# Adding scaled scan states with accumulating transfers instead of GpSimd additions, in a one-core two-layer block kernel

## The reference, cut to what matters

```
dA  = exp(delta[..., None] * A)            # 512 tokens x 512 channels x 16 states
dBu = (delta * u)[..., None] * B_ssm[:, :, None, :]
h   = dA_i * h + dBu_i                     # along the tokens
y   = einsum('bds,bs->bd', h, c_i)         # sum over the 16 states, each scaled by C
y   = y + u * D_param
```

## Time and profile before

| | |
|---|---|
| time, median of 3 runs | 3368.53 us (3368.17 to 3368.85) |
| profiled execution, its own time | 3364.8 us |
| its span, first to last instruction | 3362.8 us |
| granted TensorE clock, mean share of full speed | 0.928 |
| batches with the scan | from about 150 to 2700 us |
| expert part | from about 2785 us to the end |

### The profile page before, as it was taken

One profiled execution on the slowest core, in us unless ns is written; L12 is line 12 of the kernel. 1 busy time (PEld: TensorE's weight loads), 2 busy tenths in 40 slices (PEclk: granted clock), 3 DMA queues, 4 the chain that ended last, 5 costly groups with the idle time before them and its releaser, 6 DMA issues. The chain is left out here.

```text
span 3362.8 us, 46770 instructions
## 1 busy us (share of the span) xinstructions
PE 2834.9 (84%) x12696; PEld 1870.1 (56%) x12697; DVE 2546.5 (76%) x4108; ACT 2064.1 (61%) x3786; POOL 2592.0 (77%) x2474
## 2 busy tenths in 40 slices
PE   3686979797979797888888888888887779999998
PEld 2444555555555555555555555565545447777776
DVE  3498989899989989898999898989897842222222
ACT  3576677676767676766767676767665514444443
POOL 1399898989889898989898989898999913444444
PEclk7897989898989898989999999999998889999999
DMA  2001111111111111111110101010112313333333
GB/s 75 23 32 32 36 44 36 43 39 39 39 39 41 38 39 40 46 33 46 34 51 26 51 29 51 29 48 31 43 36 82 101 56 58 63 63 63 62 62 52
DMA packets 113898, 155.37 MB, mean 46 GB/s; under 512 B 15472, under 2 KB 73264, under 8 KB 113712
## 3 DMA queue, kind: packets, MB, share of 16 engines
q1 hardware_dynamic: 77344, 109.32, 10.4%
q0 software_dynamic: 25728, 34.75, 6.4%
q10 hardware_dynamic: 10640, 9.09, 0.8%
HBM read 107.36 MB, written 45.76 MB: 46 GB/s over the span
## 5 line engine op out<-in xcount | busy, mean ns | idle before, releaser
L872 POOL TENSOR_TENSOR dbu<-du,bbc 128x512 f32<-128x512 f32 x1024 | 1294.2, 1279 | 74.5 <-DVE h L1440 67.8
L1440 DVE TENSOR_TENSOR_SCAN h<-bank,dbu 128x512 f32<-128x512 f32 x1024 | 1227.3, 1212 | 158.7 <-ACT bank L1082 101.9
L1082 ACT ACTIVATE bank<-region,amat 128x512 f32<-128x512 f32 x1024 | 703.6, 691 | 313.3 <-DVE h L1440 299.0
L665 PE MATMUL bank<-ident,h 128*128 128x128 f32 x4096 | 624.9, 289 | 259.5 <-DVE acc L1430 231.4
L665 PEld LDWEIGHTS bank<-ident,h 128*128 128x128 f32 x4096 | 495.6, 148 | 544.3 <-DVE acc L1430 224.7
L858 POOL TENSOR_TENSOR acc<-acc,hTc 128x512 f32<-128x512 f32 x480 | 609.6, 1271 | 103.7 <-ACT hTc L1066 102.1
L1607 POOL DMA_INDIRECT out<-ye,ids x136 | 213.3, 1569 | 347.1 <-DMA out<-ye,ids 311.3
L1066 ACT ACTIVATE hTc<-bank,cT 128x512 f32<-128x512 f32 x480 | 327.3, 682 | 236.6 <-PE bank L665 236.5
L1430 DVE SCALAR_TENSOR_TENSOR acc<-bank,cT,acc 128x512 f32<-128x512 f32 x544 | 395.0, 730 | 38.9 <-PE bank L665 33.4
L619 PE MATMUL bank<-x4T,w_su 128*128 128x512 f32 (+1 forms) x768 | 389.2, 610 | 10.7 <-DVE score L1305 10.7
L1643 DVE SCALAR_TENSOR_TENSOR gg<-gt,bank 128x352 f32<-128x352 f32 x136 | 70.7, 520 | 382.2 <-ACT gt L1577 382.2
(11 more groups left out here) (204 smaller groups left out, 4361.1 us busy)
## 6 DMA issues: line engine op xcount, KB each, us to landing
bbc<-b_scratch SPq DMA_DIRECT2D x256, 256.0 KB, 3.1
xe<-slots_in SPq DMA_DIRECT2D x136, 129.0 KB
region<-in_x SPq DMA_DIRECT2D x16, 512.0 KB, 3.8
out<-x ACTq DMA_DIRECT2D x16, 512.0 KB, 3.1
region<-in_e_gu SPq DMA_DIRECT2D x8, 704.0 KB, 5.4
out<-ye,ids POOLq DMA_INDIRECT x136
slots_in<-dbu SPq DMA_DIRECT2D x16, 129.0 KB, 3.2
slots_in<-x,pos POOLq DMA_INDIRECT x128
```

Of the source, the lines that this page charges most:

```text
L665: last = tr(scan[f"hT{s}.{t}"][:, m * P:(m + 1) * P], h[:, s % 2, m, t * P:(t + 1) * P], ident[:, :])
L872: g.tensor_tensor(dbu[:, n % 4, :], du[:, m, :], bbc[:, (b * NS + s) % NROW, :], ALU.mult).then_inc(S("dbu_ready"), 1)
L1082: f(db(n)[:, :], delta[:, 1 - par, m, :], ACT.Exp, scale=amat[:, m, s:s + 1]).then_inc(S("da_ready"), 1)
L1440: v.tensor_tensor_scan(h[:, s % 2, m, :], db(n)[:, :], dbu[:, n % 4, :], 0.0, ALU.mult, ALU.add)\
```

## The change

Each of POOL's 30 additions per batch becomes a transfer from `hTc` to `acc` with `accum_op=ALU.add`. POOL issues it, the DMA engines read both and write the sum. Its completion adds 16 to one of two semaphores, one per `hTc` buffer, in place of the single counter `acc_added`. Every wait for an addition is turned into a wait for the landing of its transfer; the same engines wait at the same places.

```diff
+        acc_added = [sem(f"acc_added{k}") for k in range(2)]
+        PER_BUFFER = [(len(POOLED) + 1 - k) // 2 for k in range(2)]
+
+        def added(eng, b, k):
+            count = b * PER_BUFFER[k % 2] + k // 2 + 1
+            eng.wait_ge(acc_added[k % 2], 16 * count)
...
             elif (s - 1, t) in POOLED:
-                done(eng, "acc_added", b, POOLED.index((s - 1, t)))
+                added(eng, b, POOLED.index((s - 1, t)))
...
                     if m == 0:
                         done(pe, "acc_ready", b)
-                        done(pe, "acc_added", b)
+                        for k in range(2):
+                            pe.wait_ge(acc_added[k], 16 * (b + 1) * PER_BUFFER[k])
...
                     done(pool, "scaled", b, k)
                     acc_before(pool, b, s, t)
-                    g.tensor_tensor(acc[:, t, :], acc[:, t, :], hTc[:, k % 2, :], ALU.add).then_inc(S("acc_added"), 1)
+                    g.dma_start(acc[:, t, :], hTc[:, k % 2, :], accum_op=ALU.add).then_inc(acc_added[k % 2], 16)
...
                     scan.filled(act, f"hT{s}.{t}", b)
-                    before(act, "acc_added", b, k - 1)
+                    if b + k // 2:
+                        act.wait_ge(acc_added[k % 2], 16 * (b * PER_BUFFER[k % 2] + k // 2))
```

More of the change, by code:

```diff
@@ L272, in layers @@
                    b_stored=1, cT_ready=1, da_ready=UNITS, dbu_ready=UNITS,
-                   scan_done=UNITS, acc_init=TT, acc_ready=len(KEPT), scaled=len(POOLED), acc_added=len(POOLED), y3_ready=MC,
+                   scan_done=UNITS, acc_init=TT, acc_ready=len(KEPT), scaled=len(POOLED),  y3_ready=MC,
                    x3_ready=2, x4_ready=1, x4T_ready=DC, lexp_ready=1, sg1_ready=1, sg_ready=1, tag_ready=1, pos_ready=1, tok_set=1, weight_set=1,
```

## The result

The changed kernel takes 3411.24 us (median of four, 3405.77 to 3416.89) where the one before, measured alongside (median of four), takes 3368.69 us: the ratio is 1.0126, 95% interval 1.0111 to 1.0142, 42.6 us slower. The forecast had the direction and the range, but three times the loss (3500 us). The nearest of its cases is the rival "cheap issue, landing as forecast", 3395 us.

What follows compares the result with a forecast made beforehand. POOL was taken to bound the kernel in half of a batch's time. Profiled 3364.8 + 82 (issues) + 50 (batch ends) = 3497 us, with the median's 3.7 us offset 3500 us, 4% slower; range 3370 to 3660 us.

Steps and rivals of the forecast that it cites:

- cheap issue, landing as forecast: Rival: POOL's issue costs 1.13 us with gap, batch-end wait stays: -24 + 50 = +26 us, 3395 us; chance 0.17.
- a microsecond more or less on POOL passes by about a half: POOL taken as the bound in half of a batch's time, so half of any POOL change reaches the end.
- The price of an issue: POOL's transfer issue: 1.57 us with gap against 1.23 us per addition, 10.2 us more per batch, half passing, +82 us.
- the first rival: Cheap issue (1.13 us with gap) and quick landing (3.1 us), faster: only -24 us remain, 3345 us; chance 0.13.
- should rise or stay: Sign to look for: POOL's busy time in the batches rises or stays, not falls.
- Landing, 4.9 us: Time from POOL's issue to the transfer's landing: 4.9 us, ends 3.1 and 7.5 us.
- Ours has twice the bytes, so I add another 1.25 us: Landing step: 1.25 us added to the 3.5 or 4.0 us of the expert part's accumulating transfers.
- Waits in the middle of a batch, nothing: ACT refills an hTc buffer 7.9 and 7.4 us after the addition's start, beyond a 4.9 us landing: no cost.
- The end of the batch, 50 us: Copy 29 waits for transfer 27, DVE's last addition waits for transfer 29: 3.1 us per batch, 50 us.
- alike in all batches: Batch end: the short distances, such as 1.96 us from addition 27 to copy 29, taken as the same in every batch.
- The number and order of all other instructions are unchanged, also nothing: All instructions other than the replaced additions: no cost.
- DMA engines 60%, nothing: DMA engines in the batches: from 13% to about 60% busy at 2.5 us per transfer, B-row delay costed at nothing.

Runs made afterwards that it cites:

- x1: Kernel before, with a small power of 128 x 4 elements added on POOL behind every second addition: 3505.57 us, 1.0405 of the kernel before.
- x2: x1 with the edit of e1 (router's slot numbers in PSUM): 3474.05 us, 1.0310 of the kernel before.
- e6: Changed kernel with the 30 additions per batch left out, no transfer in their place: 3339.16 us, 0.9910 of the kernel before.
- e4: Changed kernel with the edits of e1 and e3 together: 3363.22 us, 0.9987 of the kernel before.
- e7: Changed kernel with plain copies in place of accumulating transfers (sum is wrong): 3375.71 us, 1.0023 of the kernel before.
- e1: Changed kernel with the router's slot numbers in PSUM, so DVE's multiplication has one SBUF operand: 3382.66 us, 1.0044 of the kernel before.
- c1: Control: the edit of e1 made in the kernel before: 3367.82 us, 0.9999 of the kernel before.
- e3: Changed kernel with the last four of a batch's 30 additions back on POOL's arithmetic: 3384.35 us, 1.0046 of the kernel before.

## Why the prediction was right or wrong

**The bound, "a microsecond more or less on POOL passes by about a half".** About right upward, wrong downward. Added work passes at 0.56 (x1; 0.43 without the multiplication, x2), removed work at 0.05 (e6), since DVE's 2288 us stay. The reading failed at its start: that POOL is the busier engine in half of the slices doesn't make it the one waited for, and the earlier trace rows already held a better measure, the 41.1 us that DVE waited for POOL (e6 gave 30). The text itself said "freeing POOL alone is worth little", and then used one share for both signs.

**The price of an issue, "they are accumulating, as ours are, and so the nearest row": the term that failed.** Forecast 1.57 us with the gap, measured 0.91 us by the ends (0.58 us start to start), under the lower end of 1.13 too: the next product's row starts inside the issue's row. So POOL got 30 x (1.23 - 0.91) = 9.6 us less per batch, not 10.2 us more; in place of +82 us stands a relief, of which with both losses repaired 4 us remain (e4, which keeps 26 of the 30). Accumulation does have a price, 0.33 us by the ends (e7), but that is a third of the distance from the plain copy's 0.58 us to the expert part's 1.57 us; whether its row numbers or its destination in memory make the rest wasn't run. (Of the expert part's transfers only `out` is in HBM; `ye` is in SBUF, where the first rival has both ends in HBM.) Of the signs that the prediction named, POOL's busy time fell where it "should rise or stay", and the rows' mean of 1041 ns is under its 1.2 to 1.6 us, though not under the 1.0 us at which it would have called the term wrong.

**Landing, 4.9 us.** Measured 3.4 us in the median, by the lower end of 3.1. The step "Ours has twice the bytes, so I add another 1.25 us" failed: the transfer occupies the engines 1.52 us, not 2.5, against the 1.25 us of half the bytes in the earlier trace rows. Both have 144 packets (3456 / 24 there), so in these two the time went with the packets more than with the bytes. Three transfers close together at the batch's end, however, needed 4.1 to 6.0 us in the batches that wait, so the value was nearly right at the place where it was used, in those batches.

**Waits in the middle of a batch, nothing.** Right for 15 batches, but for one wait of 0.55 us. ACT waited 22 times for a transfer, 29.9 us in all, 14 of them in the pairs at batch ends and one at the end of the last batch. Six, of 1.2 to 3.1 us, stand inside the last batch, from 2627 to 2678 us. There the weights of the expert part are loaded, the DMA engines are 88% busy (2620 to 2690 us), and the transfers land after 6.0 us (median). e3, which keeps these transfers, still has 12.3 us of such waits.

**The end of the batch, 50 us.** Mechanism right in each link (copy, transfer 29, DVE's addition). Size 26.9 us (e3). The prediction took the distances as "alike in all batches" from one batch end; they aren't, and only 7 of the 16 show the full chain.

**"The number and order of all other instructions are unchanged, also nothing": the step that was missing.** The order did not change, the time at which they meet did. DVE's multiplication of 64 elements took 2.27 us, worth 28.6 us (e1, with c1 as its control). The prediction gave no reason for the "nothing", although the sum of the masks, 917 ns before, was a sign of what such a meeting costs. The rule of the Trainium skill that was named above makes it possible, and wasn't weighed.

**DMA engines 60%, nothing.** 42%, since a transfer occupies them 1.52 us ((27.8% - 6.4%) x 3404 / 480) and not 2.5. Nothing: right, but for the last batch (e4).

**The sum.** The forecast's 132 us were 82 us of a term with the wrong sign and 50 us of one twice too large, and a term of 29 us was missing. Measured singly, the losses are 28.6 + 26.9 = 55.5 us, and what e4 gains, 4.1 us, is the relief that is left when both are repaired (3363.22 against the 3367.36 us of the kernel before that was measured with it). That makes 51.4 us where 42.6 were measured; the 8.8 us between are of the size of the uncertainty. That the direction came out right, and the time in a range of 290 us, is in part luck: with the measured 0.91 us in place of 1.57, the prediction's own sum has 30 x (0.91 - 1.23) x 0.5 x 16 = -77 us for POOL and gives 3342 us, faster than before and below the range. The two errors on POOL, price and share, happened to put a loss where the stall had been left out.

Open: why DVE's instruction waits through an issue and a product instead of getting in between them, as it did before, where it had started near a boundary as well; why the ends of POOL's rows fall behind their starts behind an accumulating issue, and which of the two prices, 0.58 or 0.91 us, holds POOL's next work; whether the 0.3 us by which transfers start later behind their scaling copy (0.07 us before) adds anything; and why the times of the four runs of the changed kernel form two pairs, 3406 and 3417 us.

## What to carry to other kernels

Before work is moved off an engine that shares the bound, run the kernel once without that work: here it would have said 30 us for 590 us removed, about the most that any way of moving it could bring. When POOL's rhythm changes, look at the rows of every DVE instruction with two SBUF operands, however small, and when an addition becomes a transfer, look at the places where its buffer is needed again within a landing time: with these two repaired, the changed kernel was a little ahead of the one before (0.9987).

## What was not expected of the hardware

- A 64-element DVE multiplication with both operands in SBUF took 0.31 us in the mean before, 2.27 us after the change and 3.67 us with POOL loaded more (x1), and 0.21 us with one operand in PSUM (e1).
- An accumulating transfer of 256 KB between two SBUF buffers occupies the DMA engines 1.52 us, a plain one (16.2% - 6.4%) x 3374 / 480 = 0.69 us; the 6.4% is this queue in the kernel before. It has 144 packets ((94848 - 25728) / 480) where the plain one has 80.
- POOL can start its next product 0.6 us into the row of an accumulating issue; the cost read from the ends of the products is 0.91 us, from their starts 0.58 us, and not the row's mean of 1.04. For a plain copy's issue both readings give 0.57 to 0.58 us.
